# A transformer decoder layer on one core: the first norm in two pairs, and the order of the first splits

## What is computed

```
x = x + attention(layernorm(x))              # 16 heads of 32, no mask, four equal ring steps = one softmax
x = x + cross_attention(layernorm(x), ctx)   # causal, keys and values from a 128-wide context
x = x + ffn(layernorm(x))                    # 512 -> 2048, gelu, 2048 -> 512

def _layernorm(x, eps=1e-05):
    m = mean(x); v = var(x)
    return (x - m) / sqrt(v + eps)

q = hidden_states @ wq.T + bq                # and k, v likewise
```

## Time and profile before

| | |
|---|---|
| median of 3 runs | 1127.78 us (1127.57 to 1129.01) |
| the profiled execution | 1128.1 us, span of its instructions 1126.3 us |
| busy, share of the span | PE 97%, PEld 68%, DVE 60%, ACT 42%, POOL 40% |
| mean DMA rate over the span | 98 GB/s |

### The profile page before, as it was taken

How to read it: one execution, slowest core, us unless ns; L and a number is a source line. 1 busy time by engine, 2 the same in 40 slices (tenths; PEclk the granted TensorE clock), 3 DMA queues, 4 the chain that set the end, 5 groups by cost and what they waited for, 6 DMA issues and landing times.

```text
span 1126.3 us, 15752 instructions
## 1 busy us (share of the span) xinstructions
PE 1092.6 (97%) x5712; PEld 764.0 (68%) x5712; DVE 678.1 (60%) x1302; ACT 476.6 (42%) x792; POOL 454.0 (40%) x414
## 2 busy tenths in 40 slices
PE   5899999999999999999999999999999999999998
PEld 4656666666666655665666666657878887887886
DVE  5686767676667678778777787845443223224112
ACT  4275555446555665645655566551221111111110
POOL 1147544444456766455647577762010001001000
PEclk9999999999999999999999999999999999999999
DMA  6843333243335446345545455302301000001001
GB/s 233 284 128 117 95 118 82 92 127 111 94 94 146 140 132 162 114 123 162 151 136 172 132 148 178 95 1 84 95 18 38 1 1 37 0 0 38 1 1 38
DMA packets 73736, 110.29 MB, mean 98 GB/s; under 512 B 6976, under 2 KB 45888, under 8 KB 71744
## 3 DMA queue, kind: packets, MB, share of 16 engines
q1 hardware_dynamic: 70864, 102.00, 30.3%
q0 software_dynamic: 2080, 6.82, 2.2%
q10 hardware_dynamic: 720, 0.54, 0.1%
HBM read 71.58 MB, written 37.75 MB: 97 GB/s over the span
## 4 chain that ended last, share of the span: by engine, by line
PE 86%; POOL 5%; ACT 4%; DVE 2%; issue 2%; DMA 1%; DVEq 0%; SPq 0%; ACTq 0%; POOLq 0%
PE PS L1081 18%; PE PS L1082 18%; PE PS L1083 18%; PE PS L1220 11%; PE PS L1204 9%; PE PS L1187 9%; POOL P_sum L866 3%; PE PS L1207 1%; ACT PT L1000 1%; PE PS L1111 1%; PE PS L1215 1%; ACT stackQ L982 1%; POOL P_sum L872 1%; DMA raw<-wkv2T 1%; POOL oTL L855 1%
## 5 line engine op out<-in xcount | busy, mean ns | idle before, releaser
L1000 ACT ACTIVATE PT<-PS 128x512 f32<-128x512 f32 (+1 forms) x432 | 228.7, 590 | 152.8 <-PE PS L1204 65.9
L866 POOL TENSOR_TENSOR P_sum<-PT 128x512 f32<-128x512 f32 x128 | 161.8, 1284 | 242.5 <-ACT PT L1000 234.8
L1433 DVE TENSOR_REDUCE m_cols<-PS 128x1 f32<-128x512 f32 x256 | 165.0, 685 | 60.7 <-PE PS L1187 59.9
L1187 PE MATMUL PS<-stackK,stackQ 96*128 96x512 f32 (+3 forms) x512 | 164.3, 378 | 4.7 <-ACT PT L1000 1.7
L1520 DVE CAST hidH<-hid 128x512 fp32r<-128x512 f32 x64 | 30.5, 477 | 225.0 <-ACT hid L1053 222.9
L1053 ACT ACTIVATE hid<-PS,b1c 128x512 f32<-128x512 f32 x64 | 43.9, 687 | 279.1 <-PE PS L1083 277.1
L1204 PE MATMUL PS<-stackQ,stackK 100*128 100x512 f32 (+3 forms) x512 | 160.0, 382 | 1.9 <-ACT stackQ L982 1.5
L872 POOL TENSOR_TENSOR P_sum<-P_sum,PT 128x512 f32<-128x512 f32 x112 | 141.7, 1287 | 6.4 <-ACT PT L1000 2.0
L1439 DVE CUSTOM_DVE_ANT_0 PS<-PS,mask_qk 128x128 f32<-128x128 f32 (+3 forms) x256 | 120.0, 518 | 36.4 <-PE PS L1187 36.3
L1447 DVE RECIPROCAL P_sum<-PS 128x512 f32<-128x512 f32 x32 | 107.5, 3358 | 47.4 <-PE PS L1220 47.0
L1204 PEld LDWEIGHTS PS<-stackQ,stackK 100*128 100x128 f32 x512 | 91.5, 191 | 55.6 <-ACT stackQ L982 25.4
(11 more groups left out here) (124 smaller groups left out, 1753.8 us busy)
## 6 DMA issues: line engine op xcount, KB each, us to landing
scratch<-stage SPq DMA_DIRECT2D x128, 256.0 KB, 2.9
stackK<-scratch SPq DMA_DIRECT2D x62, 256.0 KB, 3.9
stackQ<-scratch SPq DMA_DIRECT2D x46, 256.0 KB, 3.9
stackQ<-scratch SPq DMA_DIRECT2D x18, 512.0 KB, 4.8
stackK<-scratch SPq DMA_DIRECT2D x60, 128.0 KB, 4.1
stackQ<-scratch SPq DMA_DIRECT2D x28, 128.0 KB, 3.6
PT<-wT SPq DMA_DIRECT2D x3, 1024.0 KB, 8.9
x_res<-x SPq DMA_DIRECT2D x3, 1024.0 KB, 8.2
```

Source lines behind the costliest of these rows:

```text
L866: pool.tensor_tensor(P_sum[:, h, :], PT[:, h, :], PT[:, 4 + h, :], ALU.add).then_inc(p_added, 1)
L1000: nc.scalar.activation(PT[:, slot:slot + heads, q0:SEQ], PS[:, BANK["T", u, i], 0:heads * width].rearrange("p (h n) -> p h n", h=heads), A ...
L1187: mm = nc.tensor.matmul(dst[:, a, :], stackQ[0:STACK, par, h + a, q * P:(q + 1) * P], stackK[0:STACK, par, h + a, 0:n], start=a == 0, stop ...
L1433: nc.vector.tensor_reduce(m_cols[:, q, STACK + h:STACK + h + heads], bank, AX.X, ALU.max).then_inc(s_done, 1)
```

## The change

DVE makes statistics and aggregates for token tiles 0 and 1, and then for 2 and 3, with the small memset in each pair. POOL makes `veps` and `rstd` of two columns for each pair, with two new semaphores (`first_veps`, `first_rstd`) for the first. DVE's norms 0 and 1 wait for the first pair, norms 2 and 3 for the second. On ACT and DVE, one part of the query weights is split between token tiles 1 and 2, and the other three come behind token tile 3. The numbers of DMAs, matmuls and splits stay the same.

```diff
+        first_veps = sem("first_veps")
+        first_rstd = sem("first_rstd")
...
-            root(0)
+            for pair in range(2):
+                cols = slice(2 * pair, 2 * pair + 2)
+                pool.wait_ge(mv_done, 2 * pair + 2)
+                pool.tensor_tensor(veps[:, cols], mv[:, cols, 1], epsc[:, cols],
+                                   ALU.add).then_inc(veps_done if pair else first_veps, 1)
+                pool.wait_ge(veps_done if pair else first_veps, 1)
+                pool.tensor_tensor(rstd[:, cols], veps[:, cols], mhalf[:, cols],
+                                   ALU.pow).then_inc(rstd_done if pair else first_rstd, 1)
...
-            def high_weight(m, buf):
+            def high_weight(m, buf, parts=range(KT)):
                 act.wait_ge(w_loaded[m], DMA)
-                for k in range(KT):
+                for k in parts:
...
-            high_weight(WQ, PT[:, 0:4, :])
+            high_weight(WQ, PT[:, 0:4, :], (0,))
             high_xT(0, 2)
             high_xT(0, 3)
+            high_weight(WQ, PT[:, 0:4, :], (1, 2, 3))
...
             def first_moments():
-                for t in range(KT):
-                    if t % 2 == 0:
-                        dve.wait_ge(x_loaded[t // 2], DMA)
-                    norm_stats(t, 0)
-                norm_aggregate(0)
+                for pair in range(2):
+                    dve.wait_ge(x_loaded[pair], DMA)
+                    for t in (2 * pair, 2 * pair + 1):
+                        norm_stats(t, 0)
+                    dve.wait_ge(stats_done, 2 * pair + 2)
+                    nc.vector.memset(spare[:, :], 0.0).then_inc(spare_done, 1)
+                    for t in (2 * pair, 2 * pair + 1):
+                        nc.vector.bn_aggr(mv[:, t, :], stats[:, t, :]).then_inc(mv_done, 1)
 
             def normed(b, t, first_row):
-                if t == 0:
+                if t == 0 and isinstance(b, int) and b == 0:
+                    dve.wait_ge(first_rstd, 1)
+                elif t == 0 or t == 2 and isinstance(b, int) and b == 0:
                     dve.wait_ge(rstd_done, b + 1)
...
             low_weight(WQ, PT[:, 0:4, :], 0)
-            low_weight(WQ, PT[:, 0:4, :], 1)
-            for t in (2, 3):
-                low_xT(0, t)
-                low_weight(WQ, PT[:, 0:4, :], t)
+            low_xT(0, 2)
+            low_xT(0, 3)
+            for k in (1, 2, 3):
+                low_weight(WQ, PT[:, 0:4, :], k)
```

## The result

The changed kernel took 1123.12 us (median of 6 runs, 1121.62 to 1126.06), the kernel before 1127.89 us (6 runs, 1127.57 to 1129.01): a ratio of 0.9955, 95% interval 0.9944 to 0.9966, so 4.8 us or 0.45% faster. The forecast was 1124.4 us. The profiled execution took 1122.64 us with a span of 1120.8, 5.5 us less than the span before. One thing stands out at once: the six times spread over 4.4 us, those of before over 1.4.

What follows compares the result with a forecast made beforehand. TensorE is busy nearly throughout, so gains come from its idle time before the first projection: 1.54 plus 1.96 less 0.1 gives 3.4 us. 1128.1 us becomes 1124.7, less 0.3 for the median 1124.4; range 1122.7 to 1126.2 us.

Steps and rivals of the forecast that it cites:

- rival (b): First eight projection matmuls partly or all at high clock: 0.5 to 1.6 us more gained, 1122.8 to 1123.9 us; chance 0.30.
- The path: Whatever moves TensorE's first projection matmul moves all that follows, so the 3.4 us are kept to the end.
- The pairs: Norm statistics in two pairs of token tiles: norm 0 starts at 8.20 instead of 9.74 us, 1.54 us earlier.
- The order: Three query-weight splits moved behind token tile 3 on ScalarE and VectorE: first projection 1.96 us earlier.
- The held norm: VectorE's norm 1 held by GpSimd's second pow beside it: loss of 0 to 0.19 us, taken as 0.1 us.
- What is late next: Later weight splits keep ahead of TensorE's projections; ScalarE's first Q stage is 0.1 us late, off the path.
- The clock: TensorE's low clock over the first projections assumed as long as before; 1.6 us more gained if it stays up.
- case (a): Low clock at the first projections as before: 1124.4 us, own range 1123.8 to 1125.0 us; chance 0.45.
- (c): First pair gains nothing, transposes start at 10.5 us as before; only 1.95 us remain, 1125.8 us; chance 0.10.
- (d): A later wait in the first unit, fixed by a transfer, stops some or all gain: 1125.6 to 1127.8 us; chance 0.11.
- (e): Slower: TensorE's low clock lasts longer, 7.5 us more eating the 3.4 us gained; chance 0.04.
- a low clock beyond 18 us: Sign in the profile after that would show the prediction wrong: TensorE at the low clock later than 18 us.

Runs made afterwards that it cites:

- filled kernels: Extra identity transposes put into TensorE's idle times: the kernel before so changed took 1125.96 us, the changed kernel 1122.27 us, 1122.09 us when run again.

## Why the prediction was right, and where it wasn't

*The number.* The measured 1123.12 us lies 1.3 us below the forecast and below the forecast's own 1123.8 to 1125.0 us; it is in the range of rival (b). That the first profiled execution was one without a low stretch was chance: the next one of the same kernel took 2.4 us more.

*The path.* Right. What counts is when the first projection starts, and the clock behind it; the 1086 us behind M follow within a microsecond in every profile without a low stretch there.

*The pairs.* Forecast 1.54 us. From the start of the second moments to that of norm 0 it took 3.13 us before (6.61 to 9.74) and takes 1.49 (6.46 to 7.95): 1.64 us. The rest of the 1.79 us in the two traces is that the second moments start 0.15 us earlier in that execution, as x was there sooner, which belongs to no part. Another 0.12 us came from norm 0 to the first transpose: 0.78 us before, 0.66 in the changed kernel (7.95 to 8.61 us) and with the pairs alone (8.75 to 9.41 us). The first norm of before took a tenth of a us longer than the other three, which the forecast carried over; why it did, these runs don't separate. So the pairs gave 1.76 us.

*The order.* Forecast 1.96 us. From the first transpose to S it was 7.21 and is 5.24 us: 1.97 us, in the changed kernel and with the order alone. Together 3.7 us instead of 3.5. The medians of the filled kernels differ by 3.7 us too; that the tenth agrees is luck, given their spread.

*The held norm.* Wrong in its direction, harmless in its size. The 0.1 us taken off for it was not paid: VectorE's norms had started first, and it was GpSimd's add and pow that were lengthened. The row late in the trace, on which the term rests, is the opposite case, GpSimd's add being under way when the norm came. The lock of the Trainium skill ("SBUF — State Buffer", "SBUF: two separate sides") goes to whoever starts first, and both rows agree with that; the prediction applied it one way only. That the other is blocked in full, as that section also has it, the late row doesn't bear out: the norm ended 0.28 us after the add, while one alone takes 0.54 us (1026.18 us in the same trace). Norm 2, behind the longer pow, had to start by 9.55 us (8.61 + 1.72 - 0.78) and did at 9.52: the cover held, with nothing to spare.

*What is late next.* Right: TensorE ran from 13.85 us on without a gap; ScalarE took up the first Q at 18.51 us, as soon as it was free, and the output weights came 0.34 us late where 0.8 us of lead had been forecast, with nobody waiting behind them.

*The clock.* Here the step that failed is "the forecast assumes the low stretch is as long as before, its nearest row". There is no such length: in the unfilled profiles it lasted 0, 3.0, 3.1, 3.5 and 5.7 us from S on, and the same program showed 0, 3.1 and again 0 in three executions. The likeliest case (a) and rival (b) are not two outcomes but two kinds of execution of one kernel. The first profile is case (b) in full, 1.55 us (M - S of 20.53 for 22.08). The question behind (b), whether the clock stays up over the shorter idle time, also missed a case: in three of the profiles it had not risen before S. And the 1.00 at 14.2 us, which the prediction holds against the rule of the Trainium skill, is by itself no sign of a risen clock, since the row has 1.00 from the start of the trace; only the fall to 0.50 at 17.8 us shows that the clock had been up.

In the medians, the change is worth 4.8, 4.3 and 5.7 us in the three groups of runs that hold it unfilled, and 3.7 us with both sides filled; the 0.6 to 2 us between them would be the clock's, but the medians don't settle a microsecond. That the clock gives more to the changed kernel because its idle time is shorter is argued, not shown: the order alone has the same short idle time, and its median was no better than that of the pairs alone.

*Rivals (c), (d) and (e).* None of them came: norm 0 at 7.95 us, no gap behind S, and no low stretch of over 5.7 us at S. One of the prediction's own signs of being wrong did come in one execution, a low clock beyond 18 us: the changed kernel's second profile had it again from 37.6 us on, and its stretch behind M took 1.0 us more.

## What to carry to other kernels

A start-up chain is worth as much as it delays the first instruction of the engine that never rests again; find the copies or splits that stand ahead of the last thing it waits for, and move behind it those that are asked for part by part. Split a small serial step (here moments, root, norm) where the data arrive in parts anyway. Before a spread is put down to a change, run the kernel before as often: six runs of it spread over 1.4 us here, 29 over 5.2 us. Where TensorE's clock changes near the start, split an execution into parts (here S, M - S, and the rest) and take what a change gives from the distances between rows; work that fills TensorE's idle times can take the clock out of the times, but see in the profile that it did.

## What the runs showed of the hardware

- The granted clock's row has 1.00 from the start of the trace, but transposes at 8.6 us took 3.65 us for 16, the low rate. In these traces a level is recorded only from its first change on; durations tell the truth: 0.63 us a matmul at 1.2 GHz, 0.39 at 2.4 GHz.
- Transposes do raise the clock. In the changed kernel with 26 of them ahead, the first 18 took 3.55 us and the next 8 took 1.09 us, the high rate (16 at the low one took 3.65), before any other work of TensorE. The Trainium skill, "TensorE: Matmul & The Clock Gate", Part 4, says that they don't count; these rows contradict it.
- An idle time of 1.8 us in the middle of dense work was followed by a low stretch of 3.4 us (at 430 us), one of 1.41 us at the same place wasn't; two of 1.6 us ahead of M were followed by a low stretch in two profiles, though not in the others. The Trainium skill, "TensorE: Matmul & The Clock Gate", Part 1, says that the watch on TensorE's activity, which sets the clock, runs freely and isn't reset when a kernel starts, and that the point of the change therefore varies. That fits these profiles, where the first rise in the unfilled kernels came anywhere from before 13.7 to 22.3 us; no run here shows the watch itself.
- GpSimd's pow took 1.02 us for four columns and 0.71 for two.
